# Gating cut in two, its second half at the end of the step, in a transformer layer on one NeuronCore

## What is computed

```
xn = layernorm(x)
x + attn(xn) + ffn(xn)

attn: 16 heads of width 8, q and k rotated by position, scores with a decay bias,
      causal mask, softmax over 256 keys, times v, times Wo
ffn:  n1 = layernorm(xn) ; rw = gating(n1, smha_sim, smha_gates)            # 8 experts
      q, k, v = sum_e rw[:, e] * (n1 @ {q,k,v}_proj[e]) ; causal softmax attention, one head
      hs = xn + sum_e rw[:, e] * (attention @ o_proj[e])
      n2 = layernorm(hs) ; rw2 = gating(n2, moe_sim, moe_gates)
      hs + sum_e rw2[:, e] * (gelu(n2 @ w1[e]) @ w2[e])

gating(h, sim, gates): logits = normalize(h) @ normalize(sim) - sigmoid(gates)
      gated = relu(logits) ; experts with gated > 0, or the top 2 where none is
      softmax of gated over these
```

## Time and profile before

| | |
|---|---|
| median of 3 runs | 1437.25 us (1434.04 to 1440.95) |
| the profiled execution | 1432.54 us |
| its span, first to last instruction | 1430.7 us |
| mean granted TensorE clock | 0.984 |
| PE busy | 1284.3 us (90%) |
| DVE, ACT, POOL busy | 1021.5 (71%), 762.4 (53%), 221.6 us (15%) |
| one step in the middle, `qst<-mT` issue to `qst<-mT` issue | 702.62 to 736.79: 34.17 us |

### The profile page before, as it was taken

How to read it: one execution, slowest core, us unless ns; L and a number is a source line. 1 busy time by engine, 2 the same in 40 slices (tenths; PEclk the granted TensorE clock), 3 DMA queues, 4 the chain that set the end, 5 groups by cost and what they waited for, 6 DMA issues and landing times.

```text
span 1430.7 us, 33751 instructions
## 1 busy us (share of the span) xinstructions
PE 1284.3 (90%) x10686; PEld 1016.5 (71%) x10780; DVE 1021.5 (71%) x3882; ACT 762.4 (53%) x1664; POOL 221.6 (15%) x326
## 2 busy tenths in 40 slices
PE   0369999999999999999999999999999979999999
PEld 0247777777778777777777777777777767777776
DVE  8557777777777777777777777777776656677754
ACT  1125655665555555555555555555555574455532
POOL 4011112111122211111111111112111200000000
PEclk9679999999999999999999999999999999999999
DMA  4423233223333333333222233223223204554344
GB/s 117 94 54 85 76 77 76 75 76 80 79 85 79 78 76 79 83 90 90 77 75 76 75 83 80 76 75 76 75 76 77 58 9 172 204 202 153 149 153 159
DMA packets 89904, 133.33 MB, mean 93 GB/s; under 512 B 9675, under 2 KB 78395, under 8 KB 78523
## 3 DMA queue, kind: packets, MB, share of 16 engines
q1 hardware_dynamic: 89298, 132.10, 32.6%
q10 hardware_dynamic: 488, 0.01, 0.0%
HBM read 108.76 MB, written 21.50 MB: 91 GB/s over the span
## 4 chain that ended last, share of the span: by engine, by line
PE 63%; DVE 15%; DMA 11%; issue 6%; ACT 4%; DVEq 1%; SPq 0%; ACTq 0%
DMA qst<-mT 10%; PE ps L1663 8%; PE ps L1649 8%; PE ps L1401 7%; PE ps L1402 6%; PE ps L1411 6%; PE ps L1275 4%; PE ps L1379 4%; DVE mx L1025 3%; PE ps L1337 3%; PE ps L1360 3%; PE ps L1333 2%; PE ps L1330 2%; PE ps L1436 1%; PE ps L1383 1%
## 5 line engine op out<-in xcount | busy, mean ns | idle before, releaser
L629 ACT ACTIVATE pr<-ps 128x512 f32<-128x512 f32 x384 | 227.7, 593 | 205.4 <-PE ps L1360 166.7
L1025 DVE TENSOR_REDUCE mx<-ps 128x2 f32<-128x512 f32 (+1 forms) x384 | 263.9, 688 | 46.6 <-PE ps L1330 26.2
L634 ACT ACTIVATE ps<-trn 128x512 f32<-128x512 bf16 x382 | 229.8, 601 | 12.1
L530 POOL TENSOR_TENSOR n1s<-rep,n1T 128x256 f32<-128x256 f32 x256 | 177.0, 730 | 277.4 <-DVE mpart L1037 252.9
L1663 PEld LDWEIGHTS ps<-w2s,ats 128*128 128x128 f32 x1024 | 131.7, 192 | 50.4 <-issue 46.5
L1401 PE MATMUL ps<-n1s,wq 128*128 128x256 f32 x512 | 160.6, 396 | 0.0
L1402 PE MATMUL ps<-n1s,wk 128*128 128x256 f32 x512 | 152.8, 380 | 0.0
L1411 PE MATMUL ps<-wv,n1s 128*128 128x128 f32 x1024 | 150.6, 280 | 0.0
L803 ACT ACTIVATE n1s<-ps 128x512 f32<-128x512 f32 x128 | 76.5, 597 | 123.3 <-PE ps L1649 122.1
L1411 PEld LDWEIGHTS ps<-wv,n1s 128*128 128x128 f32 x1024 | 131.9, 192 | 9.0 <-issue 6.3
L1663 PE MATMUL ps<-w2s,ats 128*128 128x128 f32 x1024 | 135.7, 276 | 1.1 <-DVE ats L1207 1.1
(11 more groups left out here) (225 smaller groups left out, 2281.6 us busy)
## 6 DMA issues: line engine op xcount, KB each, us to landing
rep<-scr_rw SPq DMA_DIRECT2D x32, 1024.0 KB, 5.0
qst<-scr_rw SPq DMA_DIRECT2D x16, 1024.0 KB, 6.5
kst<-scr_rw SPq DMA_DIRECT2D x16, 1024.0 KB, 8.3
scr_parts<-parts SPq DMA_DIRECT2D x64, 192.0 KB, 2.3
qst<-scr_parts SPq DMA_DIRECT2D x192, 64.0 KB
kst<-scr_parts SPq DMA_DIRECT2D x32, 192.0 KB
xt<-in_x SPq DMA_DIRECT2D x32, 128.0 KB, 2.3
kst<-scr_parts SPq DMA_DIRECT2D x32, 128.0 KB
```

Of the source, the lines that this page charges most:

```text
L530: pool.tensor_tensor(n1s[:, e], rep[:, par, e], n1T[:, par], ALU.mult).then_inc(n1s_done, 1)
L629: act.activation(pr[:, G % 2, i], ps[:, S2[k % 2]], ACT.Exp).then_inc(exp_done, 1)
L634: act.activation(ps[:, S2[k % 2]], seeds[:, 1 if (k + 2) % 3 == 2 else 0], ACT.Copy).then_inc(seed_done, 1)
L1025: dve.tensor_reduce(mx[:, min(i, 1), h:h + n], ps[:, S1[k % 2]].rearrange("p (h t) -> p h t", h=n), AX_X, ALU.max, negate=True).then_inc(s ...
```

## The change

`gating` is cut into `gating_head` (L969 to L976) and `gating_tail` (L978 to L1006); the code of both is the old one. In the steps with n_x of 2 or 3 the head stays where the gating was, with row maxima 4, 5, 6 and `normalise(n, 0)` among its links, and the tail goes to the step's end behind `add_x`, with `add_hs` placed at link 24. The rest of the DVE work (the last of the layer norm, `soft_max`, maxima 7 and 8, `soft_norm`, maxima 9, 10, 11) follows the head directly. `weights_T(n+1)` now comes in the next step behind `qk(n, 1)`, into bank PVB instead of S1[1]; ACT copies the weights behind its second exponential; SP stores them right before it spreads them, behind the loads of x. `max_T` comes ahead of `soft_av`, `evac_max` ahead of `evac_v`, and SP's `put_max` follows `stacks` directly. In step NB-2 (n_x = 1) `layer_norm2(0)` is run in one piece between maxima 6 and 7. In set-up only batch 0's weights are transposed and stored; batch 1's are in step 0.

```diff
-GATE_MAX_AT = (3, 7, 10, 14, 18, 21, 24)
+GATE_MAX_AT = (3, 7, 10)
+HS_AT = 24
...
# SP, step(n, u, n_x)
                 if n_x:
+                    store_weights(n + 1, 1 - u)
                     spread_weights(n + 1, 1 - u)
                 if n_x >= 2:
                     store_parts(n + 2, u)
                 if n_x >= 2:
                     stacks(n + 2, u, True)
-                    store_weights(n + 2, u)
                 if n_x:
                     put_max(n + 1, 1 - u)
...
# ACT
-                act.activation(rwT[0:E * T, 0:P], ps[0:E * T, S1[1], 0:P], ACT.Copy).then_inc(rwT_done, 1)
+                act.activation(rwT[0:E * T, 0:P], ps[0:E * T, PVB, 0:P], ACT.Copy).then_inc(rwT_done, 1)
...
                 for k in range(3):
                     exps(n, k, n_x == 0)
+                    if n_x and k == 1:
+                        evac_weights(n + 1)
...
                 evac_ve(n)
-                if n_x >= 2:
-                    evac_weights(n + 2)
-                    evac_v(n + 2, u)
                 if n_x:
                     evac_max(n + 1)
+                if n_x >= 2:
+                    evac_v(n + 2, u)
                 evac_att(n)
...
# DVE
                 dve.tensor_tensor(Dm, L, bc(m1), ALU.subtract).then_inc(tanh_in, 1)
+                return c
+
+            def gating_tail(c, b, nt, q, groups):
...
                 dve.wait_ge(tanh_in, b + 1)
                 c.link(dve.scalar_tensor_tensor(A, Dm, 0.0, rk, ALU.is_ge, ALU.mult))
...
-                def beside_gating(k):
+                def beside_head(k):
                     next(norm, None)
                     if k in GATE_MAX_AT:
                         next_max(4 + GATE_MAX_AT.index(k))
+                    if k == 12:
+                        normalise(n, 0)
+
+                def beside_tail(k):
+                    if k == HS_AT:
+                        add_hs(n, u)
...
                 if n_x >= 2:
                     rotate(n + 2, beside_rotation)
                     next_max(3)
-                    gating(n + 2, T, 0, gate1, LG1, NORM1, 1, beside_gating)
+                    c = gating_head(n + 2, T, 0, gate1, LG1, NORM1, beside_head)
                     run(norm)
+                elif n_x:
+                    for k in range(7):
+                        next_max(k)
+                    run(norm)
+                if n_x == 1:
+                    normalise(n, 0)
+                if n_x:
+                    soft_max(n)
+                    next_max(7)
+                    next_max(8)
+                    soft_norm(n)
+                    next_max(9)
+                    next_max(10)
...
                 next_max(11)
                 if n_x:
                     max_parts(n + 1)
...
                 add_x(n, u)
-                add_hs(n, u)
+                if n_x >= 2:
+                    c.beside = beside_tail
+                    gating_tail(c, n + 2, T, gate1, 1)
+                else:
+                    add_hs(n, u)
...
# PE
-            def weights_T(b, old):
+            def weights_T(b):
                 pe.wait_ge(rw_out, 3 * (b + 1))
-                if old:
-
-                    pe.wait_ge(s1_read, UNITS * b)
-                else:
-                    pe.wait_ge(rwT_done, b)
-                pe.transpose(ps[0:E * T, S1[1], 0:P], gt[:, 6, 0:T].rearrange("p i e -> p (i e)"), ident[:]
+                if not isinstance(b, int) or b:
+
+                    pe.wait_ge(xa_done, b - 1)
+                pe.transpose(ps[0:E * T, PVB, 0:P], gt[:, 6, 0:T].rearrange("p i e -> p (i e)"), ident[:]
                              ).then_inc(rwT_out, 1)
...
# unit1
-                if k == 1:
-
-                    pe.wait_ge(rwT_done, b + 1 if not isinstance(b, int) or b else 2)
...
# pv, G == 0
+                    pe.wait_ge(rwT_done, min(n + 2, NB) if isinstance(n, int) else n + 2)
...
                 qk(n, 1)
+                if n_x:
+                    weights_T(n + 1)
...
                 out_T(n, 1)
+                if n_x:
+                    max_T(n + 1)
                 soft_av(n, (lambda: pe.wait_ge(lg_read, f + 1)) if n_x >= 2 else (lambda: None))
                 if n_x >= 2:
-                    weights_T(f, True)
                     proj_v(f, True)
-                if n_x:
-                    max_T(n + 1)
```

More of the change, by code:

```diff
@@ L447, in _ @@
             stacks(1, 1, False)
-            store_weights(1, 1)
             put_max(0, 0)
@@ L779, in _ @@
                 gate_tanh(b)
-                evac_weights(b)
+                if b == 0:
+                    evac_weights(b)
             evac_max(0)
@@ L953, in rotate, with gate_views, bc, gating_head @@
                 c.close()
-            def gating(b, nt, which, q, lg, norm, groups, beside=None):
+            def gate_views(nt):
+                def bc(v):
+                    return v.rearrange("p (t o) -> p t o", o=1).broadcast_to((P, nt, E))
+                return bc, [gt[:, k, 0:nt] for k in range(6)], [gs[:, k, 0:nt] for k in range(6)]
+            def gating_head(b, nt, which, q, lg, norm, beside=None):
                 chain, lg_out, lg_read, tanh_in, tanh_out, rwT_out, rw_out = q
                 c = Chain(dve, chain, b, GATE_LINKS, beside)
[L960 to L966, removed]
+                bc, (L, Dm, A, B2, C2_, F), (m1, m2, mc, rn, ina, tot) = gate_views(nt)
                 sgb = sg[:, which:which + 1].broadcast_to((P, nt, E))
@@ L976, in gating @@
                 dve.tensor_tensor(Dm, L, bc(m1), ALU.subtract).then_inc(tanh_in, 1)
+                return c
+            def gating_tail(c, b, nt, q, groups):
+                chain, lg_out, lg_read, tanh_in, tanh_out, rwT_out, rw_out = q
+                bc, (L, Dm, A, B2, C2_, F), (m1, m2, mc, rn, ina, tot) = gate_views(nt)
+                th = gt[:, 9, 0:nt]
+                rk = rank[:].rearrange("p (o e) -> p o e", o=1).broadcast_to((P, nt, E))
                 dve.wait_ge(tanh_in, b + 1)
@@ L1009, in gating @@
                 c.close()
+            def gating(b, nt, which, q, lg, norm, groups, beside=None):
+                gating_tail(gating_head(b, nt, which, q, lg, norm, beside), b, nt, q, groups)
             LG1 = ps[:, G0, 0:T * LG_W].rearrange("p (i k) -> p i k", k=LG_W)
@@ L1147, in beside_gating, with beside_last @@
                         next_max(4 + GATE_MAX_AT.index(k))
+                    if k == 12:
[3 more added lines that the diff above has]
+                        add_hs(n, u)
+                def beside_last(k):
                     if k == 12:
@@ L1156, in step @@
                     next_max(3)
-                    gating(n + 2, T, 0, gate1, LG1, NORM1, 1, beside_gating)
+                    c = gating_head(n + 2, T, 0, gate1, LG1, NORM1, beside_head)
                     run(norm)
-                else:
[L1160 to L1166, removed]
-                    else:
-                        for k in range(1, GATE_LINKS + 1):
-                            beside_gating(k)
-                        run(norm)
+                elif n_x:
[11 more added lines that the diff above has]
+                    next_max(10)
+                else:
+                    run(norm)
+                    gating(0, BP, 1, gate2, LG2(0), LG2(0)[:, :, E], 2, beside_last)
+                    run(layer_norm2(2))
                 next_max(11)
@@ L1617, in _ @@
                 proj_v(b, False)
-                weights_T(b, False)
+                if b == 0:
+                    weights_T(b)
             pe.wait_ge(set_dma, 16 * (N_SMALL + N_ROWS))
```

## The result

The changed kernel took 1451.26 us (median of 4 runs, 1447.92 to 1454.55), the kernel before 1436.13 (4 runs, 1434.04 to 1440.95): ratio 1.0098, 95% interval 1.0072 to 1.0124. It is slower by 1.0%, outside the predicted range, and on the side to which the prediction gave 0.12. The profiled execution's span is 1446.1 us against 1430.7: 15.4 us more.

What follows compares the result with a forecast made beforehand. PE, busy 90%, was bound by gaps waiting for the maxima's DMA and a row maximum. 30 x (0.45 - 0.11) + 29 x 0.1 - 2.1 = 11.0 us gave 1426.3 us; own range 1418 to 1434, 8 in 10 1404 to 1440.

Steps and rivals of the forecast that it cites:

- the side to which the prediction gave 0.12: Whole kernel: slower by more than 0.5%, 7.2 us; chance 0.12.
- part 2: `weights_T` and the tail at the step's start: costs 0.11 us of PE per step, idle DVE time covers the tail.
- the sign of a failed placing: At the step's start: PE waiting at L1308 for L1006 would show that the placing of the tail had failed.
- Part 1: Tail out of the step's middle: 0.66 us gained at unit 10, 0.21 lost at unit 9, gain 0.45 per step.
- the moved stall, rival two: Middle of the step: unit 9 waits 0.45 us instead of 0.21, landing gains nothing; 1436 us, chance 0.18.
- Part 3: `max_T` ahead of `soft_av`, `weights_T` gone from there: PE only arrives 0.22 us earlier at the DMA wait, gain 0.
- Part 4: `put_max` issued at about z+4.7 instead of z+6.66: landing stays at z+11.5, gain 0.1 us from the 8 KB gone.
- The first rival: Maxima's DMA lands within 3 us of issue, PE never waits, 1.28 us more gained per step; 1392 us, chance 0.13.
- Part 7: Step NB-2, once: `layer_norm2(0)` in one piece makes PE stand at unit 9; loss 2.1 us with `weights_T`.

Runs made afterwards that it cites:

- e1: The changed kernel with DVE's hardware loop over steps 2 to 27 written out: 1428.4 us, ratio 0.9952 to the kernel before.
- e2: The kernel before with DVE's hardware loop written out: 1427.0 us, ratio 0.9947 to the kernel before.
- e3: The kernel before with only the maxima's part of the change, their DMA issued earlier: 1433.3 us, ratio 0.9993 to the kernel before.
- e4: The changed kernel with the maxima's DMA issued from ACT instead of SP: 1453.6 us, ratio 1.0125 to the kernel before.
- e8: The kernel before with k's half of the stacks and the weights' store issued behind the maxima's DMA: 1398.9 us, ratio 0.9743 to the kernel before.
- e7: The changed kernel with k's half of the stacks issued behind the maxima's DMA: 1440.7 us, ratio 1.0042 to the kernel before.
- e6: The changed kernel with four steps instead of two in a pass of DVE's loop: 1454.1 us, ratio 1.0128 to the kernel before.

## Why the prediction was wrong, and where it was right

**The step that failed is in part 2**: "So the 2.18 and 2.46 us of idle DVE time cover the tail." The 2.46 us before L942 were read as DVE waiting for PE, since the row names PE. In every second step they were also the branch, whose standstill alone takes 2.7 to 3.0 us. Filled with the tail, DVE comes to the branch 2.5 us later, at +2.1 behind `unit2(0)` instead of -0.4, and it lies open: rotation at +5.5 instead of +2.7 us, second projection 0.95 us later, z 0.82 us later, 12 times: 9.8 us. No rival named it either, though the kernel text shows the loop, and the trace of before had the branch laid open in steps 6, 10 and 12, once under the name "issue". e1 against e2 gives what the same placing costs without the branch as long as PE waits for the DMA: +1.4 us, within the noise.

The tail itself was placed well. The working had it end near 743.6, 1.8 us behind `unit2(0)`; L1014 starts 1.95 and 2.01 us behind it in the two steps shown.

What the prediction offered as the sign of a failed placing, PE waiting at `weights_T` for the tail, did not come: L1335 waited for L1014 in set-up, 11.1 us, and else for 0.2. PE came to stand a little further on, at the second projection. The order tail, branch, rotation was the path, and only its first part had been priced.

**Part 1** had the right mechanism and too much gain. Maximum 8 no longer holds L1333 (now L1357: 3.5 us of weight loads' wait), but L1350 and L1354, which are unit 9, took over with 13.2 and 11.6 us: some 0.36 us lost there by starts, not 0.21. In the changed kernel `soft_max` runs from 701.75 to the next instruction at 702.68, 0.93 us instead of 0.74. So the gain was near 0.1 to 0.2 us a step, where 0.34 were taken; the moved stall, rival two, was the nearer account of this part. The steps between the branches gained 0.1 us each.

**Part 3** holds: nothing.

**Part 4** holds in what decides it: the landing hangs on z (e3, and 7.50 us from issue to landing). The gain of 0.1 us from the 8 KB did not show. Its reason, "they stand behind the stacks' data", is right in the order and wrong if read as SyncE's queue alone (e4). The first rival had the right size for the DMA's term in the kernel before: 29 x 1.28 = 37.1 us, and e8 gains 37. For the changed kernel it had not, since e7 gains 10.5.

**Part 7** sized step NB-2 about right, 1.65 us where 2.1 were taken, and placed it wrongly: PE stood at `pv(2)`, not at unit 9.

**The range** does not come out of its own bounds. With the stall between 0 and 0.45 and the landing's gain between 0 and 0.3 us, the forecast's formula gives 1414 to 1436 us, not 1418 to 1434; the measured 1451 is outside both. And 0.66 us times 31 is 20.5, near the 20.7 of the earlier trace rows, but that row counts 38 waits.

**A term that was missing**: DVE's tail takes longer in its new place. The lines L986 and L988 of the changed kernel (count, then min/median/max ns):

```profile
L986 DVE SCALAR_TENSOR_TENSOR gt<-gt,rank x40: 174/767/783, 48.5 to 1394.5; 128x16 f32<-128x16 f32 x32, 128x64 f32<-128x64 f32 x8
```

```profile
L988 DVE TENSOR_TENSOR gt<-gt,gs x40: 224/445/486, 48.9 to 1395.0; 128x16 f32<-128x16 f32 x32, 128x64 f32<-128x64 f32 x8
```

The median of L986 is 767 ns; as L978 in its old place it was 175. That of L988 is 445, where L980 had 303. Together they took 21 us more in the whole program, half of the 41 us by which DVE's busy time grew. GpSimd's `scale` runs there, from 639.88 to 645.40. Links L986 to L995 take 2.8 us instead of the 1.9 of part 2, and `add_hs` with them is later. The reduce L987 between the two, with one input, stays at 170, and L991 and L992, which have two and start behind 645.40, take 174 and 175. The Trainium skill, page "GPSIMD Engine Reference", section "Specifications", says that DVE instructions with two SBUF inputs contend with GpSimd; these lines agree. It was seen, not tried: no run moved `scale` away, so how much of the loss it carries is open.

## What to carry to other kernels

An idle stretch of an engine that lies across the back edge of its hardware loop is not free: part of it can be the loop's branch, while the wait's name says something else, since only the last to end is named. Before filling it, ask what the engine does there when nothing waits, and look at a step without a branch beside one with it. And where a small DMA is late behind large ones, change what is issued ahead of it: neither an earlier issue nor another issuing engine helped here, and moving 384 KB behind it took 2.6% off the kernel before.

## What the hardware showed that I had not expected

- A taken back branch of DVE's loop costs 2.7 to 3.4 us of standstill with two steps in a pass (before and after) and 3.8 to 4.4 with four (e6), with three packets of instruction DMA around each; not taken, 0.07 us.
- Code written out is quicker than the loop in steps without a branch too: 0.4 us in a step of 34 (e2), the cause open.
- A 128x16 DVE instruction with two SBUF inputs took 767 ns beside GpSimd's products where it took 175 elsewhere.
- 24 KB issued from ACT landed at the same z+11.8 us as from SP, with the DMA engines busy 49.7% of the first 2.9 us behind its issue from ACT, in which none of its packets started.
